# A softmax's row of maxima, written as eight rows by VectorE; and a new order of the work between the graph weights and head 0

## What is computed

```python
diff = c_adj[:, None, :] - c_adj[:, :, None]
A = jnp.abs(jnp.abs(jax.nn.sigmoid(diff) - 0.5) - 0.5) * 2.0
Wg = adj[None, :, :] * A_s                      # A_s: A made symmetric
g = jnp.einsum('bcn,bnm->bcm', fea, Wg)
g = jax.nn.relu(g * para.reshape(1, C, N))
q = jnp.transpose(g, (0, 2, 1)).reshape(B, N, h, hd).transpose(0, 2, 1, 3)
kv = (x @ kv_w).reshape(B, N, 2, h, hd).transpose(2, 0, 3, 1, 4)
k, v = (kv[0], kv[1])
attn = jax.nn.softmax(jnp.einsum('bhnd,bhmd->bhnm', q, k) * scale, axis=-1)
out = jnp.einsum('bhnm,bhmd->bhnd', attn, v)
...
x = _layernorm(x + _L0_gnn_ref(x, L0_gnn_para, adj, L0_gnn_kv_w), axis=-1)
```

## Time and profile before

| | us |
|---|---|
| median of 3 runs | 2867.29 (2865.73 to 2867.63) |
| the profiled execution | 2866.0 |
| its span, first to last instruction | 2864.0 |

### The profile page before, as it was taken

One profiled execution on the slowest core, in us unless ns is written; L12 is line 12 of the kernel. 1 busy time (PEld: TensorE's weight loads), 2 busy tenths in 40 slices (PEclk: granted clock), 3 DMA queues, 4 the chain that ended last, 5 costly groups with the idle time before them and its releaser, 6 DMA issues. The chain is left out here.

```text
span 2864.0 us, 39358 instructions
## 1 busy us (share of the span) xinstructions
PE 2711.2 (95%) x12436; PEld 1850.8 (65%) x12436; DVE 1988.9 (69%) x2859; ACT 1663.1 (58%) x2146; POOL 1279.5 (45%) x684
## 2 busy tenths in 40 slices
PE   7999999999999999999999999996799999989964
PEld 5565665656656566665656656563688888878854
DVE  6687786877878687786877878784633333348878
ACT  6566576766667666576666767653422222237768
POOL 3755647565474755657566474745200000000025
PEclk9999999999999999999999999998899999999976
DMA  4123222232222232222232222220332223305556
GB/s 136 60 84 101 74 66 84 63 106 84 66 73 77 73 97 86 73 66 85 64 105 86 65 72 77 84 71 30 120 104 88 88 94 107 108 16 190 190 229 256
DMA packets 126943, 272.01 MB, mean 95 GB/s; under 512 B 11952, under 2 KB 62128, under 8 KB 123312
## 3 DMA queue, kind: packets, MB, share of 16 engines
q1 hardware_dynamic: 126896, 271.42, 29.4%
HBM read 178.79 MB, written 62.98 MB: 84 GB/s over the span
## 5 line engine op out<-in xcount | busy, mean ns | idle before, releaser
L303 POOL TENSOR_TENSOR psum<-psum,probs 128x1024 f32<-128x1024 f32 x320 | 784.3, 2451 | 144.2 <-ACT probs L373 118.1
L373 ACT ACTIVATE probs<-sc_ps 128x1024 f32<-128x1024 f32 x512 | 508.0, 1024 | 410.4 <-PE sc_ps L822 328.9
L552 DVE TENSOR_REDUCE mx<-mx_ps 128x1 f32<-128x512 f32 x768 | 520.2, 690 | 275.3 <-PE mx_ps L791 273.5
L838 PE MATMUL pv_ps<-probs,v 128*64 128x512 f32 x2048 | 492.4, 604 | 0.0
L822 PE MATMUL sc_ps<-qa,ka 128*128 128x512 f32 x1024 | 387.4, 404 | 0.0
L822 PE MATMUL sc_ps<-qb,kb 128*128 128x512 f32 x1024 | 380.6, 394 | 0.5
L791 PE MATMUL mx_ps<-ka,qa 128*128 128x512 f32 x768 | 315.4, 424 | 10.2 <-DVE mx L552 2.9
L838 PEld LDWEIGHTS pv_ps<-probs,v 128*64 128x64 f32 x2048 | 125.6, 136 | 224.5 <-issue 193.6
L822 PEld LDWEIGHTS sc_ps<-qa,ka 128*128 128x128 f32 x1024 | 187.5, 188 | 106.2 <-issue 64.1
L791 PEld LDWEIGHTS mx_ps<-ka,qa 128*128 128x128 f32 x768 | 139.8, 187 | 179.6 <-issue 77.9
L1177 DVE TENSOR_TENSOR agg_lo<-ag_ps,agg_hi 128x1024 fp32r<-128x1024 f32 x32 | 39.2, 1225 | 310.7 <-ACT agg_hi L1104 310.7
(11 more groups left out here) (195 smaller groups left out, 5548.2 us busy)
## 6 DMA issues: line engine op xcount, KB each, us to landing
adj_ring<-in_adj_dram SPq DMA_DIRECT2D x128, 512.0 KB, 3.7
pre_scratch<-pre SPq DMA_DIRECT2D x28, 1024.0 KB, 4.4
pre<-pre_scratch SPq DMA_DIRECT2D x28, 1024.0 KB, 4.9
x<-in_x_dram SPq DMA_DIRECT2D x16, 1024.0 KB, 5.6
kb<-ka SPq DMA_DIRECT2D x64, 256.0 KB, 3.1
res<-in_x_dram SPq DMA_DIRECT2D x16, 1024.0 KB, 5.6
x_scratch<-res SPq DMA_DIRECT2D x16, 1024.0 KB, 4.5
x1s<-x_scratch SPq DMA_DIRECT2D x16, 1024.0 KB, 7.5
```

Of the source, the lines that this page charges most:

```text
L303: pool.tensor_tensor(psum[:, h % 2, :], probs[:, 0, :] if k == 1 else psum[:, h % 2, :], probs[:, k % PR, :], ALU.add).then_inc(s["pool_ad ...
L373: nc.scalar.activation(probs[:, i % PR, :], sc_ps[:, t % 2, :], ACT.Exp, scale=SCALE)\
L552: nc.vector.tensor_reduce(mx2[:, nh, n:n + 1], mx_ps[:, nh, :], AX.X, ALU.max)\
L838: ins = nc.tensor.matmul(pv_ps[nh * HD:(nh + 1) * HD, h % 2, :], v[:, i, h * HD:(h + 1) * HD], probs[:, i % PR, nh * BANK:(nh + 1) * BANK] ...
```

## The change

- `maxima_row` writes `qb[h]` itself. It reads the transposed maxima (8 x 128 in PSUM) eight times side by side, multiplies by -1 and by the 8 x 8 identity (each of its columns spread over 128), and writes eight rows of 1024: row t holds the negated maxima of tile t in the columns of that tile, and zero elsewhere. `kb` gets eight rows of ones instead of one. `row`, `store_row` and its semaphore `row_in` are gone; `scores` waits for `row_done`.
- Head 0's transposed maxima lie in the second half of `sc_ps`, so that only tile 1's scores have to wait for `row_done`.
- The last step of `g_product` signals `g_first` for each half of block 0. `q_times_para` works block 0 in these halves, and ScalarE rounds the first half apart (`q_first`).
- TensorE's order between the weights and head 0 is new, with the values first; `v_product` can be cut within a tile.
- ScalarE: `den_copy` stands behind tile 5's distance and tanh; `v_copy(b, 0)` stands ahead of the keys.
- `copy_kb(b, 1)` has lost its wait for `qh_done`.

The core of the diff:

```diff
@@ SyncE
-            def store_row(b, h):
-                wait(sp, s["row_done"], 4 * b + h + 1)
-                r = other(h).start
-                sp.dma_start(qb[h][r:r + 1, :].rearrange("o (t p) -> o t p", p=P).bitcast(F32),
-                             row[:, :].bitcast(F32)).then_inc(s["row_in"], 16)
@@ GpSimd, once
-                pool.memset(kb[h][one:one + 1, :].bitcast(F32), 1.0).then_inc(s["kq_set"], 1)
+                pool.memset(kb[h][one:one + T, :].bitcast(F32), 1.0).then_inc(s["kq_set"], 1)
@@ ScalarE
+            def q_first(b):
+                wait(act, s["qt_done"], 3 * b + 1)
+                nc.scalar.activation(qa[0][own(0), 0:BANK], scr[own(0), 0, 0:BANK], ACT.Relu).then_inc(s["q_first"], 1)
+
             def q_high(b, h):
-                wait(act, s["qt_done"], 2 * b + h // 2 + 1)
-                nc.scalar.activation(qa[h][own(h), :], scr[own(h), h // 2, :], ACT.Relu).then_inc(s["qh_done"], 1)
+                wait(act, s["qt_done"], 3 * b + h // 2 + 2)
+                cols = slice(0 if h else BANK, N)
+                nc.scalar.activation(qa[h][own(h), cols], scr[own(h), h // 2, cols], ACT.Relu).then_inc(s["qh_done"], 1)
@@ VectorE
             def q_times_para(b, c):
                 if c == 0:
-                    wait(dve, s["g_first"], b + 1)
-                else:
-                    wait(dve, s["g_step"], 8 * b + 8)
+                    for nh in range(NH):
+                        wait(dve, s["g_first"], 2 * b + nh + 1)
+                        cols = slice(nh * BANK, (nh + 1) * BANK)
+                        nc.vector.tensor_tensor(scr[:, 0, cols], sc_ps[:, 0, cols], neg_para[:, 0, cols], ALU.mult)\
+                            .then_inc(s["qt_done"], 1)
+                    return
+                wait(dve, s["g_step"], 8 * b + 8)
...
             def maxima_row(b, h):
                 wait(dve, s["rowT_ready"], 4 * b + h + 1)
-                wait(dve, s["row_in"], 16 * (4 * b + h))
-                src = (mx_ps if h else sc_ps)[0:T, 0, 0:P]
-                nc.vector.tensor_scalar(row[:, :], src, -1.0, None, ALU.mult).then_inc(s["row_done"], 1)
+                src = (mx_ps if h else sc_ps)[0:T, 0 if h else 1, 0:P].rearrange("t (o p) -> t o p", o=1)
+                r = other(h).start
+                diagonal = ident[0:T, 0:T].rearrange("t (u o) -> t u o", o=1)
+                nc.vector.scalar_tensor_tensor(qb[h][r:r + T, :].rearrange("t (u p) -> t u p", p=P),
+                                               src.broadcast_to([T, T, P]), -1.0, diagonal.broadcast_to([T, T, P]),
+                                               ALU.mult, ALU.mult)\
+                    .then_inc(s["row_done"], 1)
@@ TensorE
                 if 0 in parts and 0 in halves:
                     wait(pe, s["exp_done"], 32 * b + t - 1)
                     if t < 2:
-                        wait(pe, s["qt_done"], 2 * b + t + 1)
+                        wait(pe, s["qt_done"], 3 * b + t + 2)
+                    if t == 1:
                         wait(pe, s["row_done"], 4 * b + 1)
@@ TensorE, body
                 g_product(b)
-                k_piece(b, 0, 0)
-                k_piece(b, 0, 1)
-                max_scores(b, 0, 0)
-                max_scores(b, 0, 1)
-                k_piece(b, 1, 0)
-                max_scores(b, 0, 2)
-                k_piece(b, 1, 1)
-                max_scores(b, 0, 3)
                 for m in range(4):
                     v_product(b, 0, [m])
-                    max_scores(b, 0, 4 + m)
+                    max_scores(b, 0, m)
+                for k in range(4):
+                    k_piece(b, k // 2, k % 2)
+                    max_scores(b, 0, 4 + k)
                 v_product(b, 1, [0, 1])
+                v_product(b, 1, [2], (0, 3))
                 transpose_maxima(b, 0)
-
-                v_product(b, 1, [2, 3])
+                v_product(b, 1, [2], (3, 6))
+                v_product(b, 1, [3])
```

More of the change, by code:

```diff
@@ L177, in copy_kb @@
                     wait(sp, s["row_done"], 4 * b + h)
-                elif h == 1:
-                    wait(sp, s["qh_done"], 4 * b + 1)
-                else:
+                elif h == 0:
                     wait(sp, s["row_done"], 4 * b)
@@ L430, in body @@
                 w_high(b, 3)
+                distance(b, 5)
+                tanh_half(b, 5)
                 if before:
                     den_copy(b - 1, HEADS - 1)
-                distance(b, 5)
-                tanh_half(b, 5)
                 w_high(b, 4)
@@ L442, in body @@
                 w_high(b, 7)
+                q_first(b)
                 q_high(b, 0)
@@ L447, in body @@
                 q_high(b, 3)
+                v_copy(b, 0)
+                relu_q(b, 1)
+                if not last:
+                    x_high(b + 1, range(0, 3))
                 k_high(b, 2)
                 k_high(b, 3)
-                relu_q(b, 1)
                 if not last:
[L452 to L455, removed]
+                    x_high(b + 1, range(3, 6))
                 v_copy(b, 1)
@@ L537, in double_q @@
             def double_q(b):
-                wait(dve, s["qt_done"], 2 * b + 1)
+                wait(dve, s["qt_done"], 3 * b + 2)
                 nc.vector.tensor_scalar(qa[0][other(0), :], scr[own(0), 0, :], 0.0, None, ALU.max)\
@@ L729, in k_piece, with v_product @@
                     ins.then_inc(s["k_ready"], 1)
-            def v_product(b, j, tiles=range(4)):
+            def v_product(b, j, tiles=range(4), part=(0, 6)):
                 if j == 0:
@@ L737, in v_product @@
                     rows = slice((4 * j + m) * P, (4 * j + m + 1) * P)
-                    ins = product(mx_ps[:, m // 2, (m % 2) * C:(m % 2 + 1) * C], split_terms(
-                        [((xT_hi[:, k, rows], xT_lo[:, k, rows]), (kvw_hi[:, k, C:2 * C], kvw_lo[:, k, C:2 * C]))
-                         for k in range(CT)]))
+                    terms = split_terms([((xT_hi[:, k, rows], xT_lo[:, k, rows]),
+                                          (kvw_hi[:, k, C:2 * C], kvw_lo[:, k, C:2 * C])) for k in range(CT)])
+                    for k in range(*part):
+                        ins = nc.tensor.matmul(mx_ps[:, m // 2, (m % 2) * C:(m % 2 + 1) * C], *terms[k],
+                                               start=k == 0, stop=k == len(terms) - 1)
                 if m == 3:
@@ L758, in g_product @@
                                                        start=n == 0 and k == 0, stop=n == T - 1 and k == 2)
-                        if n == T - 1 and c == 0:
-                            ins.then_inc(s["g_first"], 1)
+                            if n == T - 1 and c == 0:
+                                ins.then_inc(s["g_first"], 1)
                     ins.then_inc(s["g_step"], 1)
@@ L798, in transpose_maxima @@
                     wait(pe, s["merged"], 3 * b + h)
-                out = (mx_ps if h else sc_ps)[0:T, 0, 0:P]
+                out = (mx_ps if h else sc_ps)[0:T, 0 if h else 1, 0:P]
                 nc.tensor.transpose(out, mxs[:, :], ident[:, :]).then_inc(s["rowT_ready"], 1)
@@ L813, in scores @@
                 if 1 in parts and 0 in halves and i == 0:
-                    wait(pe, s["row_in"], 16 * (4 * b + h + 1))
+                    wait(pe, s["row_done"], 4 * b + h + 1)
                     wait(pe, kb_in[h % 2], 16 * (2 * b + h // 2 + 1))
```

16 lines of the change are left out of this document (6 added, 10 removed).

## The result

| | before | after |
|---|---|---|
| median of 6 runs | 2867.38 us (2865.15 to 2867.82) | 2842.49 us (2839.77 to 2843.72) |
| span of the profiled execution | 2864.0 us | 2837.9 us |

The ratio is 0.9914, with a 95% interval of 0.9901 to 0.9927: 24.9 us faster, 1.8 us beyond the forecast of 2844.3 and inside the likeliest case (2839 to 2849).

The account below looks back on a forecast made before the run. VectorE's chain was taken as the bound, since TensorE can't get past head 1's maxima. 15 x 1.49 + 0.6 = 23 us gained gave a median of 2844.3 us; range of 8 in 10: 2835 to 2859.

Parts of the forecast that it names:

- likeliest case: Whole kernel: 1.2 to 1.8 us a batch less, 2839 to 2849 us, chance 0.52.
- block 1's L534 starts: VectorE after block 0's halves and double_q: block 1's multiplication starts at 908.5 instead of 909.82, 1.3 us earlier.
- duration of the row: VectorE, each head: the new row takes 1.23 us like L507, +0.95 us, on the path in head 0 only.
- head 1's maxima start: VectorE, end of head 0: this start moves from 924.77 to 923.28, and its 1.49 us is a batch's gain.
- The front of the chain: VectorE in the weights: waits of 1.27 and most of 0.70 us go, statistics start at 902.5 instead of 904.15.
- Rival A: Weights, tile 6: the adjacency lands late and the front stays; 0.3 us a batch, 5 us in all, 2862; chance 0.09.
- rival B: VectorE's row: contention or repeated reads make it 3.39 us; +3 us a batch, 2915 us; chance 0.05.
- the point of 2.3 us: Head 1: a row of some 2.3 us would make its row_done hold head 2's first scores.
- The hold at head 1: TensorE at head 1's approximate scores: its wait for maxima grows from 1.1 to about 2 us.
- rival C: Transfers cost latency on the path, 2740, excluded; small form, head 1's maxima held less, 2830 to 2839, chance 0.1.
- The transfers: 64 row transfers go: hidden in heads 1 to 3, costed at nothing beyond head 0, where removal is in the sum.
- The 0.6 us of batch 0: Batch 0, with no batch before it: only the halves, the order and the row count, about 0.6 us gained.

Follow-up runs that it names:

- e3: The changed kernel with den_copy back ahead of tile 5's distance and tanh, the rest as changed: 2863.62 us, ratio 0.9989.
- e5: The changed kernel with the row's instruction issued twice, the second behind the first by a semaphore: 2883.15 us, ratio 1.0051.
- e1: The changed kernel with the old 8 x 128 row and its SyncE transfer back, the new order kept: 2836.34 us, ratio 0.9895.
- e2: The kernel before, in its old order, with the new row, no transfer and copy_kb(b, 1) without its wait: 2871.59 us, ratio 1.0018.

## Why the prediction was right

It was right by its own mechanism, and its terms can be checked one by one. In us, batch 7, each as the move against before:

| step | forecast | measured |
|---|---|---|
| statistics start | -1.65 | -1.64 (891.55) |
| weights end | -0.45 | -0.51 (897.21) |
| block 1's L534 starts | -1.32 | -1.37 (897.49) |
| transposed maxima, row starts | -1.91 | -1.89 (908.61) |
| duration of the row | 1.23 | 1.22 |
| `k_low` starts | -0.97 | -1.06 (909.75) |
| head 1's maxima start | -1.49 | -1.56 (912.25) |
| period | -1.49 | -1.64 |

- **The front of the chain.** Both waits ahead of `weigh` went, 1.97 us together, and the 0.31 us for `transpose_back` came in their place, as forecast; the statistics moved by the rest. e3 shows that most of the gain hangs on this: without it the change is worth 0.2 us a batch, with the row counted in. Rival A, the adjacency's load, did not come: of all 128 `weigh` (L508, source view of after) those that waited are

```profile
  ACT scr L319: 2.9, 3
  DMA adj_ring<-in_adj_dram: 0.2, 1
```

  e3 shows what rival A would have given: 0.2 us a batch, where it had 0.3, from a 13.41 us that its text does not work out.

- **The row.** The choice of L507 as its neighbour was right, and with that rival B fell: 1.216 us at most in all 64, each with a GpSimd instruction beside it. For head 1 the point of 2.3 us from which it would hurt was about right (e5: two rows, some 2.5 us, cost 0.39 us there). For head 2 the prediction named only its idle time, and e5 shows some 0.5 us of slack.
- **The keys' start is 0.09 us earlier than forecast**, since the next instruction starts 1.14 us behind the row and not 1.23, and this is more than the 0.07 us by which head 1's maxima beat the forecast.
- **The hold at head 1** went from 1.07 to 1.92 us, forecast 1.1 to about 2. The small form of rival C therefore did not come either.
- **The transfers** were worth nothing in heads 1 to 3, as costed: the table's last three stretches are the same in e1 as in the changed kernel to 0.03 us. In head 0 their removal was in the sum, though the waits of the earlier trace rows alone could not say what they would cost in the new order. e1 says it: 0.39 us of TensorE's time in head 0, and less than the row.
- **The size.** The forecast was 15 x 1.49 + 0.6 = 23 us. Measured, 15 x 1.63 are 24.5 us, by the medians of the periods; the spans differ by 26.1 us, the medians of the runs by 24.9. The term that was too small is the one of 1.49, by 0.14 us: 0.07 are head 1's maxima, 0.09 the stretch from row 1 to row 2, which the prediction did not move at all, and 0.02 go back behind row 2. That these were small is luck, since the wait for GpSimd in head 1 was not read. The 0.6 us of batch 0 can't be told: its row starts at 65.3 before and at 63.7 after, but between 63.9 and 64.9 in the profiles of the ten experiments, whatever their order.
- **What it did not see** is that the change holds two things of opposite sign. It put the row's +0.95 us into head 0's sum, yet did not set it against the same order with the old row. The row was a loss of 5 us by the table (15 x 0.33), 6.2 by the medians: TensorE's wait for the transfer stands beside a VectorE that gets to head 1 earlier. Nor would the comparison alone have found its size: done for e1 it came to 0.15 us a batch at most.

The parts can't be added. Alone the front brings 12.3 us; taken out of the whole it costs 21.1. TensorE's order costs 15.9 us and the halves 10.5 when taken out. The timelines above suggest why: each of them removes a wait that lies right behind the one before. Two parts of the change were not run by themselves: the new place of head 0's transposed maxima, and `copy_kb(b, 1)` without its wait, which is in e2 together with the row.

## What to carry to other kernels

Moves along one chain can pay more together than each does alone: take each out of the whole as well as trying it alone, and expect the two numbers to differ. Before a transfer is traded for a longer instruction, look at which engine the next stage waits for; here the transfer ran beside other work for all but 0.39 us, and the instruction that replaced it stood on the chain that the next head waits for. When a wait goes, ask for the next one on the same engine: here it went from the transpose to GpSimd's sum, and a later place for one addition took that one too.

## What the runs showed of the hardware

- VectorE's time here went by the elements of each partition, not by the number of partitions, also where both inputs are read with repeats: 8 x 1024 out of 8 x 128 in PSUM and 8 x 8 in SBUF took 1.216 us (L561), 128 x 1024 took 1.225. Reading each input element many times cost nothing that shows beside it. The source view of after:

```profile
L561 DVE SCALAR_TENSOR_TENSOR qb<-mx_ps,ident x48: 1211/1212/1216, 82.6 to 1934.9; 8x1024 fp32r<-8x1024 f32 x48
L561 DVE SCALAR_TENSOR_TENSOR qb<-sc_ps,ident x16: 1216/1216/1216, 63.7 to 1874.3; 8x1024 fp32r<-8x1024 f32 x16
```

- The spread of these 64 is 5 ns, with a GpSimd instruction beside each of them, in 31 of them one that had begun 0.9 us or more before. L508, with both inputs in SBUF, has a median of 1.217 us and a slowest of 3.385: in the timelines of after, 30 of its 128 took 3.07 us or more, all of them begun 0.2 to 0.4 us after a GpSimd addition, and none of the 82 with no GpSimd instruction beside them. The Trainium skill ("SBUF — State Buffer", Who interferes with whom) says that a VectorE instruction with at most one input in SBUF, outside its two-port modes, does not contend with GpSimd, and that one with two such inputs contends with a GpSimd instruction that reads SBUF; the trace agrees in all 64 and in the 30.
- A small transfer from SBUF to SBUF cost 2.03 us from its issue to the matmul that waited for it, in the old order and in the new one (e1, 906.76 to 908.79). The figure of about 2.0 us that rival C cites is given in its section for transfers that GpSimd issues; this one is issued by SyncE.
